# Wider mask products in the second layer of a two-layer block, and a new order of the steps of both layers

## The reference

```python
# layer 0: x + attention(norm(x)) + soft mixture of experts(norm(x))
scores = (q @ k.T + q_rope @ k_rope.T) / scale      # 16 heads of 8, causal
w = softmax(where(causal, -inf, scores));  attn = (w @ v) @ W_o
logits = rmsnorm(x) @ rmsnorm(slots).T              # 8 experts x 64 slots
out = softmax_slots(logits) @ experts(softmax_tokens(logits).T @ x)
# layer 1: x + attention(norm(x)) + top-8 of 16 experts(norm(x)) + shared expert
att = softmax(where(causal, -inf, (q @ k.T) / 8))   # 16 heads of 64, k and v from a latent
y = (att @ v) @ w_out
h = silu(x @ w_gate.T) * (x @ w_up.T);  y += sum_e combine_e * (h @ w_down.T)
```

## Time and profile before

| | |
|---|---|
| median of 3 runs | 3098.85 us (3097.3 to 3101.01) |
| the profiled execution | 3096.49 us, of which its span is 3094.8 us |
| mean granted clock of PE | 0.984 of 2.4 GHz |
| PE busy | 2884.3 us, 93% of the span |
| DVE busy | 2310.2 us, 75% |
| ACT busy | 1802.6 us, 58% |
| POOL busy | 1314.4 us, 42% |
| DMA | mean 96 GB/s |

### The profile page before, as it was taken

One profiled execution on the slowest core, in us unless ns is written; L12 is line 12 of the kernel. 1 busy time (PEld: TensorE's weight loads), 2 busy tenths in 40 slices (PEclk: granted clock), 3 DMA queues, 4 the chain that ended last, 5 costly groups with the idle time before them and its releaser, 6 DMA issues.

```text
span 3094.8 us, 63911 instructions
## 1 busy us (share of the span) xinstructions
PE 2884.3 (93%) x23492; PEld 1512.2 (49%) x23492; DVE 2310.2 (75%) x4199; ACT 1802.6 (58%) x3771; POOL 1314.4 (42%) x1223
## 2 busy tenths in 40 slices
...
GB/s 112 59 57 54 53 72 68 54 59 56 59 52 61 68 29 131 117 119 115 120 122 116 120 122 115 121 121 115 123 119 116 122 120 115 126 117 115 118 120 69
DMA packets 271910, 297.70 MB, mean 96 GB/s; under 512 B 30832, under 2 KB 235760, under 8 KB 271088
## 3 DMA queue, kind: packets, MB, share of 16 engines
...
...
## 4 chain that ended last, share of the span: by engine, by line
PE 51%; DMA 3%; DVE 3%; issue 2%; SPq 2%; ACT 1%; POOL 0%; DVEq 0%; ACTq 0%; POOLq 0%
PE l_ps_out L1643 8%; PE l_ps_any L1543 6%; PE l_ps_any L1545 6%; PE l_ps_any L1544 6%; PE l_ps_any L1668 5%; PE l_ps_exp L1626 4%; PE l_ps_any L1675 4%; PE l_ps_exp L1628 4%; PE l_ps_any L1601 3%; DMA l_y_rec<-rec_scratch 2%; PE l_ps_sum L1654 2%; PE l_ps_exp L1630 2%; SPq L1173 1%; DVE l_neg_max L1466 1%; PE l_ps_any L1606 1%
## 5 line engine op out<-in xcount | busy, mean ns | idle before, releaser
L1260 POOL TENSOR_TENSOR l_hid<-l_hid,l_spread 128x512 f32<-128x512 f32 x256 | 327.9, 1281 | 655.1 <-DVE l_hid L1495 480.3
L1347 ACT ACTIVATE l_probs<-l_ps_exp 128x512 f32<-128x512 f32 x640 | 376.8, 595 | 211.4 <-PE l_ps_exp L1630 201.0
L673 DVE TENSOR_REDUCE neg_max<-ps_any 128x1 f32<-128x384 f32 (+3 forms) x704 | 411.0, 634 | 115.7 <-PE ps_any L800 113.7
L536 ACT ACTIVATE probs<-ps_exp 128x512 f32<-128x512 f32 x640 | 352.1, 607 | 41.5 <-PE ps_exp L815 28.4
L455 POOL TENSOR_SCALAR_AFFINE_SELECT probs<-probs 128x512 f32<-128x512 f32 x256 | 160.0, 637 | 458.9 <-ACT probs L536 457.4
L1466 DVE TENSOR_REDUCE l_neg_max<-l_ps_any 128x2 f32<-128x768 f32 (+2 forms) x384 | 316.1, 862 | 35.4 <-PE l_ps_any L1606 34.4
L1626 PE MATMUL l_ps_exp<-l_q_a,l_k_a 128*128 128x512 f16 (+3 forms) x1024 | 306.4, 300 | 10.3 <-DMA l_q_b<-l_max_row 6.5
L1643 PE MATMUL l_ps_out<-l_probs,l_v 128*64 128x512 f32 (+3 forms) x2048 | 303.9, 439 | 0.7 <-ACT l_yT L1322 0.7
L1499 DVE TENSOR_TENSOR l_hw<-l_hid,l_hw 128x512 f16<-128x512 f32 x272 | 257.9, 953 | 60.2 <-ACT l_hw L1330 60.0
L1353 ACT ACTIVATE l_hid<-l_ps_any 128x512 f32<-128x512 f32 x272 | 162.4, 597 | 236.3 <-PE l_ps_any L1545 217.9
L1628 PE MATMUL l_ps_exp<-l_q_b,l_k_b 65*128 65x512 f16 (+3 forms) x1024 | 295.2, 300 | 0.0
...
## 6 DMA issues: line engine op xcount, KB each, us to landing
l_spread<-route_scratch SPq DMA_DIRECT2D x128, 512.0 KB, 4.7
l_q_a<-l_q_hi SPq DMA_DIRECT2D x256, 128.0 KB, 2.4
l_y_rec<-rec_scratch SPq DMA_DIRECT2D x128, 256.0 KB, 4.3
l_q_b<-l_q_lo SPq DMA_DIRECT2D x128, 128.0 KB, 2.4
l_k_a<-l_k_hi SPq DMA_DIRECT2D x128, 128.0 KB, 3.2
l_k_a<-l_k_lo SPq DMA_DIRECT2D x128, 128.0 KB, 2.8
l_k_b<-l_k_hi SPq DMA_DIRECT2D x128, 128.0 KB, 2.9
...
```

The source lines that it names most:

```text
L536: nc.scalar.activation(probs[:, n % 2, u], ps_exp[:, (10 * g + u) % 3], ACT.Exp, scale=float(HD0 + DR) ** -0.5).then_inc(exp_done.sem, 1)
L673: nc.vector.tensor_reduce(neg_max[:, n % 2, heads[0]:heads[0] + k, t], src, AX.X, ALU.max, negate=True).then_inc(drained["dve"], 1)
L1260: nc.gpsimd.tensor_tensor(at, at, spread[:, c % 3, n % SPREAD], ALU.mult).then_inc(weighted.sem, 1)
L1347: nc.scalar.activation(probs[:, n % 2, u], ps_exp[:, (5 * p + u) % ST_BANKS], ACT.Exp, scale=float(HD1) ** -0.5).then_inc(exp_done.sem, 1)
```

## The change

It touches four things.

1. In `exp` of layer 1 the mask products of a bank's two blocks become one with an output of two strided blocks (`diagonals`) and a mask held twice in SBUF. Only the first product of a bank has the start flag.
2. In `max` of layer 1 the same is done for each half and each head: two products of 64 columns become one of 128. All score products of the unit come first and the masks last.
3. The first `sums` of a set waits for `rec` of the set just before it, and no longer for the one before that.
4. `ORDER0` and `ORDER1` hold the same steps in another order.

```diff
+def diagonals(columns):
+    at = [c // P for c in columns]
+    return slice(at[0], at[-1] + 1, at[1] - at[0] if len(at) > 1 else 1)
...
-        mask_h = sb("mask_h", [P, P], BF16)
+        mask_h = sb("mask_h", [P, 2, P], BF16)
...
-                    for q, t, c in MAX1[step[3]]:
+                    for k, (q, t, c) in enumerate(MAX1[step[3]]):
                         w = (t + 1) * P
                         for r, rows in sides:
                             pe.matmul(scores[r][:, c:c + w], q_hi[rows, q, t * P:t * P + P], k_hi[rows, q, 0:w],
-                                      start=True, stop=False)
-                        for half in range(2):
-                            to = c + t * P + HD1 * half
-                            for r, rows in sides:
-                                ins = pe.matmul(scores[r][:, to:to + HD1], later_h[rows, half], ident_2[rows],
-                                                start=False, stop=(half == 1))
+                                      start=(k == 0), stop=False)
+                    blocks = diagonals([c + t * P for q, t, c in MAX1[step[3]]])
+                    for half in range(2):
+                        for r in range(2):
+                            rows = slice(HD1 * r, HD1 * r + HD1)
+                            out = scores[r].rearrange("p (x h k) -> p x h k", h=2, k=HD1)[:, blocks, half]
+                            ins = pe.matmul(out, later_h[rows, half], ident_2[rows, 0:len(MAX1[step[3]])],
+                                            start=False, stop=(half == 1))
...
-                                  start=True, stop=False)
+                                  start=(c == 0), stop=False)
...
-                        ins = pe.matmul(out[:, 0:P], ident_h[:], mask_h[:], start=False, stop=True)
-                    ins.then_inc(exp_full.sem, 1)
+                    out = ps_exp[:, m % ST_BANKS].rearrange("p (x q) -> p x q", q=P)
+                    pe.matmul(out[:, diagonals([c for r, k, c in EXP1[step[3]]])], ident_h[:],
+                              mask_h[:, 0:len(EXP1[step[3]])], start=False, stop=True
+                              ).then_inc(exp_full.sem, 1)
...
-                    if j == 0 and p >= 2 * SET:
-                        pe.wait_ge(rec_ok.sem, rec_ok.at(p // SET - 1, 0))
+                    if j == 0 and p >= SET:
+                        pe.wait_ge(rec_ok.sem, rec_ok.at(p // SET, 0))
```

More of the change, by code:

```diff
@@ L145 @@
[L145 to L160, removed]
@@ new lines @@
+    ("values", 0, 0, 2), ("out_rows", 0, 0), ("dispatch", 0, 2), ("dispatch", 0, 3), ("logits_c", 0, 0),
+    ("exp", 0, 1, 6), ("load_heads", 0, 3), ("logits_c", 0, 1), ("soft_c", 0, 0), ("exp", 0, 1, 7),
+    ("soft_c", 0, 1), ("slots", 0, 0), ("max", 0, 2, 9), ("turn_rows", 0, 0), ("max", 0, 2, 10),
+    ("exp", 0, 1, 8), ("exp", 0, 1, 9), ("hidden", 0, 0), ("norm", 1, 0), ("values", 0, 1, 0), ("scale", 1, 0),
+    ("turn_max", 0, 2), ("values", 0, 1, 1), ("share_c", 0, 0), ("hidden", 0, 1), ("max", 0, 3, 0),
@@ new lines @@
+    ("exp", 0, 2, 6), ("out_rows", 0, 1), ("low_k", 1, 0), ("share_c", 0, 1), ("exp", 0, 2, 7),
+    ("turn_max", 0, 3), ("k", 1, 0), ("exp", 0, 2, 8), ("exp", 0, 2, 9), ("values", 0, 2, 0),
+    ("expert_out", 0, 0), ("exp", 0, 3, 0), ("exp", 0, 3, 1), ("share_c", 0, 2), ("exp", 0, 3, 2),
+    ("turn_rows", 0, 1), ("out_rows", 0, 2), ("values", 0, 2, 1), ("values", 0, 2, 2), ("share_c", 0, 3),
+    ("exp", 0, 3, 3), ("load_heads", 1, 0), ("exp", 0, 3, 4), ("combine", 0, 0), ("combine", 0, 1),
@@ L167 @@
+    ("turn_rows", 0, 3), ("max", 1, 1, 0), ("max", 1, 1, 1), ("max", 1, 1, 2), ("max", 1, 1, 3),
+    ("combine", 0, 2), ("exp", 1, 0, 0), ("max", 1, 1, 4), ("combine", 0, 3),
 )
@@ L920 @@
 ORDER1 = (
[L921 to L940, removed]
```

93 lines of the change are left out of this document (59 added, 34 removed).

## The result

The changed kernel takes 3193.7 us (median of 4 runs, 3192.85 to 3200.53) against 3098.8 us before: ratio 1.031, 95% interval 1.029 to 1.033. It is slower by 95 us; the prediction said faster (3069 us). Its profiled execution is the slowest of the four: it has a span of 3198.8 us at a mean granted clock of 0.971, 104 us more than the profiled one of before.

The account below looks back on a forecast made before the run. PE's queue was taken to bound the kernel. Layer 0 at -1.8 us a batch (-29 in 16) and layer 1 at 0 took 3096.5 to 3067.5, predicted 3069 against the median; range 3038 to 3102.

Parts of the forecast that it names:

- xnT's wait: Layer 0: PE's wait for xn (0.67 + 0.16 us) shrinks to 0.2, a gain of 0.6 us a batch.
- hidden 0: Layer 0: its wait for soft_c (0.53 + 0.16 us) goes, covered by slots; a gain of 0.7 us a batch.
- combine: Layer 0: new wait before combine 0 for POOL's last two shares, +0.7 us a batch (bounds 0.3 and 1.5).
- Gelu's banks: Layer 0: score products' wait for these banks (0.74 + 0.32 us) shrinks to 0.6; -0.5 us a batch.
- max 0 0: Layer 0: first max of the next batch late because k is stored later, +0.3 us a batch (bounds 0 and 1).
- rival 1: Layer 0: waits only change place, removed ones come back elsewhere; 3090 to 3100 us, chance 0.16.
- the banks of max 3: Layer 1: max 3 1 to 3 4 take the same two banks one after another, +0.6 us a batch.
- the hw steps: Layer 1: three hw on DVE before up_in, whose bank qk 1 2 takes; +0.6 us a batch (bounds 0 and 1.7).
- the prediction's last case: Layer 1: its new order gains as layer 0's does, down to 3040 us; chance 0.05.
- The masks: Layer 1's exp and max: cost follows streamed columns, so merging saves 0.2 us a batch, 3 us in 16.
- Rival 2: Layer 1: sums 0 waits for a late rec, 24 us; with layer 0's waits only moved, 3115 to 3125; chance 0.12.
- Rival 3: Layer 1: a mask product costs as such, whatever its columns; saves 33 instead of 3 us, 3039 us, chance 0.05.

Follow-up runs that it names:

- e3: Changed kernel with only rec_in 1 moved from ahead of cT to right behind turn_max 3 in layer 1's order; 3172.8 us.
- e7: As e6, with combine 0 and 1 of layer 0 moved from behind exp 3 4 to behind turn_rows 2; 3066.9 us.
- e10: As e6, with layer 0's share_c 1, 2 and 3 moved earlier, behind soft_c 2, low_q and turn_max 3; 3095.4 us.
- e13: As e7, with layer 0's q, ckv, low_q, r, k of the next batch two to four steps earlier, low_k behind k; 3159.1 us.
- e6: Changed kernel with spread_in 4 and 5 moved right behind turn_max 1 and rec_in 1 right behind turn_max 3; 3074.9 us.
- e4: Kernel before with only the merged mask products and the new wait of sums, both layers' orders as before; 3091.1 us.

## Why the prediction was wrong

**The step that failed** is in layer 1's order: "SP's queue: rec_in 1 waits for divide 1 and holds up cT's store and the row of turn_max 3; exp 6 0 has about 0.6 us to spare: nothing." The walk asked when SP issues a row, and no term of it asks how long the row then takes to land. That step is short by 1.3 us a batch at `exp 6 0` (e3: 21 us in all). SP's queue there, in one batch of the changed kernel:

```profile
2044.66 1.24 SPq L1215 DMA_DIRECT2D l_y_rec<-rec_scratch  x2
2046.09 0.45 SPq L1190 DMA_DIRECT2D route_scratch<-l_weightT  x1
2046.58 0.57 SPq L1182 DMA_DIRECT2D l_q_b<-l_max_row  x1
```

ACT's copy had ended at 2045.5, so SP holds the row up by 1.0 us, as the prediction said; but it lands after 3.7 us instead of 1.7. With 3.0 us more in all and a wait of 1.3, some 1.7 us were to spare (an estimate from these numbers): the hold alone would have cost nothing, the landing made the wait. The same question was not asked of `turn_max 1` at all, though the trace of before had PE waiting for this row already (6.5 us, left out of the earlier trace rows). There spread_in 5 had moved ahead of the row and `rec` behind the reductions of `max 1 1` and `max 1 2` as well; both can be read in the two lists, and the prediction weighs neither for the row. The late row of `turn_max 1` cost 4.7 us a batch of wait and some 2.1 of clock.

**Layer 0** forecast -1.8, measured -0.3 us a batch. Gone as said: xnT's wait and that of `turn_rows 2` for y_un; the wait of turn_max stays, as said. `hidden 0` no longer waits for soft_c, but 0.3 of the 0.7 us are left, for slotsT. Wrong by size: combine (+0.7, measured 16.1 / 14 + 0.16 = 1.3; the walk took POOL as free for the last two shares and left out `share_c 1` and the three selects, 1.81 us, that end at 594.97). Also Gelu's banks (-0.5 forecast; (8.9 + 29 x 0.16) / 14 = 1.0 us is left of 1.1), and max 0 0 (+0.3; 0.6). Four of 0.2 to 0.3 us were not foreseen (a `max`, `turn_rows 3`, a part of `combine` and an `exp`). The gaps in PE's queue, which are what lies from start to start beyond the time in which a product's columns stream, sum to 5.3 us a batch before and 4.8 after, counted from 0.15 us up over 100 to 1060 us. So rival 1, "the waits only change place", is what layer 0 did, at 0.16 of the chance, and e7, e10 and e13 show how: take one away, and the next queue is late.

**The rest of layer 1** came out better than forecast. The waits of the earlier trace rows are gone and new ones stand at the banks of max 3: (9.4 + 5.4 + 52 x 0.16) / 13 = 1.8 us against a forecast of 0.6 there and 0.6 for the hw steps, where nothing waits. Without the two late rows the new order has a period of 114.7 us (e6), 1.0 us below the old one with the same masks (e4), where the prediction's terms for the order sum to +0.2. Of that 1.0 us, 0.75 is in the gaps from 0.15 us up (2.4 in e4, 1.65 in e6). So freed of the late rows the order of layer 1 gains some 15 us, in the direction of the prediction's last case, which had 0.05 of the chance.

**The masks**: mechanism right, size 5.8 instead of 3 us (e4, interval 4 to 10); some of it is shorter waits in e4's list and not the products. **Rival 2** (sums 0 waits for rec): no row of PE waits for L1485, and e4, which has the new wait, is not slower. It named the side of the result and the lateness of `rec`, but not the path by which it acts: not through PE's `sums` but through SP and the DMA engines. **Rival 3**: out, by the pace and by e4. The range (3038 to 3102) missed since no case in it had a transfer that lands late. Its lower end is that of rival 3: the lower ends of the new waits, worked out as 16 x 1.0 us, sum to 0.4 + 0.3 + 0.6 = 1.3 us a batch, which is 21 us and ends at 3048. Nothing hung on it.
